# Splitting the first sixteen of 256 indirect embedding loads into two of 64 rows each

## What is computed

```
e = stack([tbl_f[ids[:, f]] for f in range(32)], axis=1)          # 1024 x 32 x 32
x1 = einsum('bpd,pj->bjd', outer(e, e).reshape(b, 32*32, 32), W0)  # 1024 x 128 x 32
x2 = einsum('bpd,pj->bjd', outer(e, x1).reshape(b, 32*128, 32), W1)
z = sum(concatenate([x1, x2], axis=1), axis=-1)                    # 1024 x 256
h = relu(concatenate([z, dense_ctx], axis=1) @ W_top1 + b_top1)
h = relu(h @ W_top2 + b_top2)
y = h @ W_top3
```

## Time and profile before

| what | value |
|---|---|
| time, median of 3 runs | 376.81 us (376.74 to 376.88) |
| the profiled execution: its span, first to last instruction | 597.7 us |
| the profiled execution: a time of its own, beside the span | none is recorded |
| mean granted TensorE clock in it | 0.800 |
| PE, DVE, ACT, POOL busy | 412.6, 203.4, 235.5, 246.5 us |

### The profile page before, as it was taken

The page is one execution under the profiler, slowest core; times in us unless marked ns, Lnnn a source line. Parts: engine busy times, 40 slices in busy tenths (PEclk is TensorE's granted clock), DMA queues, the critical chain, the costliest instruction groups (busy, mean ns, idle before and its releaser), DMA issues.

```text
span 597.7 us, 9512 instructions
## 1 busy us (share of the span) xinstructions
PE 412.6 (69%) x3656; PEld 360.8 (60%) x3656; DVE 203.4 (34%) x834; ACT 235.5 (39%) x774; POOL 246.5 (41%) x262
## 2 busy tenths in 40 slices
PE   5512112874257887877788778687787679999988
PEld 4301001653256776766666667577676668989988
DVE  4200000694723333322333233333332235556510
ACT  3300000662175334522343334433452237676641
POOL 6777772547055444544445554544444440000000
PEclk9755555795589877877787888977787779999999
DMA  8100000000000000000000000000000000000000
GB/s 299 45 14 13 13 13 6 11 3 14 2 10 10 8 10 7 10 8 9 9 9 10 10 10 9 11 8 9 8 10 8 8 10 2 2 2 2 2 2 1
DMA packets 10765, 9.66 MB, mean 16 GB/s; under 512 B 4664, under 2 KB 8896, under 8 KB 10720
## 3 DMA queue, kind: packets, MB, share of 16 engines
q0 software_dynamic: 8192, 4.21, 4.8%
q1 hardware_dynamic: 2528, 4.84, 2.3%
HBM read 9.03 MB, written 0.00 MB: 15 GB/s over the span
## 4 chain that ended last, share of the span: by engine, by line
PE 57%; issue 18%; another core or an unknown queue 11%; DVE 7%; ACT 6%; DMA 1%; SPq 0%; ACTq 0%
PE WA L725 20%; PE QB L697 10%; PE PA L687 8%; PE T L710 4%; DVE RT L421 4%; PE M L738 4%; PE M L757 2%; PE ET L674 2%; ACT eblk L285 2%; ACT TS L285 1%; PE PA L639 1%; PE M L764 1%; PE M L748 1%; ACT RT L285 1%
## 5 line engine op out<-in xcount | busy, mean ns | idle before, releaser
L278 POOL DMA_INDIRECT emb<-in_table,rows x256 | 245.8, 960 | 239.0 <-PE ET L674 165.3
L725 PE MATMUL WA<-TS,RX 128*128 128x128 f32 x896 | 127.0, 301 | 1.0 <-ACT TS L285 1.0
L584 DVE COPY TS<-T 32x64 f32<-32x64 f32 x256 | 55.5, 217 | 200.6 <-PE T L710 184.6
L725 PEld LDWEIGHTS WA<-TS,RX 128*128 128x128 f32 x896 | 119.7, 215 | 6.0 <-issue 6.0
L697 PE MATMUL QB<-eblk,zQ 128*64 128x68 f32 x1024 | 69.1, 243 | 74.3 <-issue 74.0
L697 PEld LDWEIGHTS QB<-eblk,zQ 128*64 128x64 f32 x1024 | 49.9, 146 | 89.8 <-issue 85.8
L552 DVE TENSOR_TENSOR zQ<-ET,eT 128x1024 f32<-128x1024 f32 x32 | 39.2, 1225 | 159.0 <-ACT eT L285 158.9
L687 PE MATMUL PA<-eblk,zP 128*128 128x132 f32 x512 | 80.6, 296 | 5.3 <-issue 3.4
L639 PE MATMUL PA<-sym,TS 128*128 128x272 f32 x64 | 29.4, 552 | 74.5 <-issue 47.3
L687 PEld LDWEIGHTS PA<-eblk,zP 128*128 128x128 f32 x512 | 73.4, 212 | 6.3 <-issue 4.9
L285 ACT ACTIVATE eblk<-ET 32x256 f32<-32x256 f32 x128 | 48.6, 380 | 71.0 <-PE ET L674 66.0
(11 more groups left out here) (87 smaller groups left out, 294.1 us busy)
## 6 DMA issues: line engine op xcount, KB each, us to landing
emb<-in_table,rows POOLq DMA_INDIRECT x256
TS<-in_W SPq DMA_DIRECT2D x8, 256.0 KB, 4.3
wt<-in_W_top SPq DMA_DIRECT2D x2, 512.0 KB
y1w<-in_W_rows SPq DMA_DIRECT2D x1, 448.0 KB
TS<-in_W_rows SPq DMA_DIRECT2D x1, 448.0 KB
sym<-in_W_cols SPq DMA_DIRECT2D x1, 264.0 KB, 2.8
TS<-in_W_cols SPq DMA_DIRECT2D x1, 264.0 KB, 3.1
idc<-in_ids SPq DMA_DIRECT2D x1, 128.0 KB, 2.0
```

The source lines that it names most:

```text
L278: eng.indirect_dma_start(emb[par][:, g, :], None, table, bass.IndirectOffsetOnAxis(rows[:, k, g:g + 1], 0))\
L584: eng.tensor_copy(view(ts[32 * q:32 * q + 32, :, :], P * REST + b0, [[4 * P, 2], [P, 4], [1, 8]]), view(src, q, [[C17, 2], [4, 4], [C33, 8 ...
L725: m = eng.matmul(WA[:, 0:P], C[:, kt, :], TS[k % 2][:, slot_of(kt), :], start=(kt == 0), stop=(kt == KT - 1))
```

## The change

The loads of the first two units (tile 0, units 0 and 1: 16 loads) are each issued as two loads of 64 rows: partitions 0 to 63 with row numbers from `rows`, and partitions 64 to 127 with row numbers from a new tile `upper`. `upper` lies on partitions 0 to 63. It is filled by a third direct load on SyncE's queue, and VectorE adds the table starts to it, behind the making of `rows`. The second load of each pair waits for that sum. Since each load adds 16 to its semaphore, TensorE's waits on these two units count 16 x 8 more.

```
+    HALVED = 2
...
+        upper = sb("upper", [P // 2, HALVED * UG], I32)
...
             eng.dma_start(base[:, :], bases).then_inc(ids_loaded, 16)
+            eng.dma_start(upper[:, :], ids[P // 2:P, 0, 0:HALVED * UG]).then_inc(upper_loaded, 16)
             eng.dma_start(sym[:, :], w0_cols[0]).then_inc(w0_loaded, 16)
...
                     for g in range(UG * unit, UG * unit + UG):
+                        if k == 0 and unit < HALVED:
+                            eng.indirect_dma_start(emb[par][0:P // 2, g, :], None, table,
+                                                   bass.IndirectOffsetOnAxis(rows[0:P // 2, k, g:g + 1], 0))\
+                               .then_inc(gathered[par][unit], 16)
+                            eng.wait_ge(upper_made, 1)
+                            eng.indirect_dma_start(emb[par][P // 2:P, g, :], None, table,
+                                                   bass.IndirectOffsetOnAxis(upper[:, g:g + 1], 0))\
+                               .then_inc(gathered[par][unit], 16)
+                            continue
...
+            eng.wait_ge(upper_loaded, 16)
+            some = view(base[0:P // 2, :], 0, [[0, HALVED * UG]])
+            eng.tensor_tensor(upper[:, :], upper[:, :], some, ALU.add).then_inc(upper_made, 1)
             eng.wait_ge(w0_loaded, 16 * 2)
...
-                eng.wait_ge(gathered[k % 2][unit], 16 * UG * (k // 2 + 1))
+                halves = 16 * UG if k % 2 == 0 and unit < HALVED else 0
+                eng.wait_ge(gathered[k % 2][unit], 16 * UG * (k // 2 + 1) + halves)
```

More of the change, by code:

```diff
@@ L141, in dlrm_cin_tower @@
         ids_loaded = sem("ids_loaded")
+        upper_loaded = sem("upper_loaded")
+        upper_made = sem("upper_made")
         w0_loaded = sem("w0_loaded")
```

## The result

The changed kernel takes 394.73 us (394.59 to 394.94, 4 runs) against 376.85 (376.74 to 377.24, 4 runs): +17.9 us, a ratio of 1.0464 (95% interval 1.0433 to 1.0495). The forecast was 389.0, with a range of 380 to 397.

What follows compares the result with a forecast made beforehand. The prediction took POOL's unbroken row of indirect loads as the bound; 16 more loads add 12.4 us to 376.8, giving 389.2, less some taken up by PE's floor: forecast 389.0, range 380 to 397.

Steps and rivals of the forecast that it cites:

- What bounds the kernel: Whole kernel: POOL's row of indirect loads without a gap sets the end, a floor of 365.0 to 369.9 us.
- unnamed rest of 6.9 to 11.8 us: What the median holds above POOL's floor: time around the span and whatever late signals a timed run has.
- The price of a load of 64 rows: POOL's 16 added loads: bounded by +4.8 and +20.0 us, middle taken, +12.4, a half load about 0.71 + 0.30.
- the likeliest case: Middle cost of a half load on POOL: range 384 to 393 us, chance 0.48.
- a half costs as much as a whole: Rival on POOL's loads: time does not depend on rows, +16.5 to 20 us, 393 to 397, chance 0.20.
- The wait, the direct load, the extra sum: Start of the kernel: wait for `upper` taken as 0, SyncE's load one issue of 0.42 us, VectorE's sum 0.
- What is late next: PE behind units 0 and 1: data 6.2 us later, PE's floor up 10.0, POOL's other 240 loads 12.4 later.
- The two floors: Ends of a run without late signals: 365.0 to 369.9 us by POOL, 363 to 383 by PE.
- Half cost: Rival on POOL's loads: only the idle pieces count, +4.8 us on POOL, 380 to 382, chance 0.16.
- Slack on POOL: Rival: late signals or profiler-made idle pieces leave POOL slack, so the change is hidden, 377 to 380 us, chance 0.12.
- the faster case: Rival on the 23 columns behind unit 0: half loads disturb PE's signals less, at best about 371 us, chance 0.04.

## Why the prediction held, and where its size was off

**What bounds the kernel.** Right, though the profile that I had could not show it directly. The sum was 324.1 for the end of the row, 0 to 4.9 for the landing, 40.9 behind it. The second profile of the same kernel has 332.7 (331.78 + 0.94), 1.4 and 40.9 (375.1 - 334.16). The 8.6 us between 324.1 and 332.7 I had left in an unnamed rest of 6.9 to 11.8 us; they are the loads slowed by VectorE's sums (8.4 us, by the run with the sums replaced). Half of that size stood in a row that I quoted: by the mean of 0.960 the 256 loads take 4.1 us more than by the median of 0.944 that I used. Another 1.8 us lie around the span. The 13 runs beside the second profile have spans of 374.7 to 376.1 us, so they leave no room for late signals such as the first profile had.

**The price of a load of 64 rows.** This is the term that was mis-sized. I had 0.71 + 0.30 and +12.4, the middle between half the cost and the whole; it is 0.903 + 0.30 and +18.6, of which 17.9 show in the time. So the likeliest case was the wrong one, and the rival "a half costs as much as a whole", with 393 to 397 and a chance of 0.20, is what happened. The stated range held the result only because it took in this rival too. By the last sentence of the prediction, which calls it wrong if a half load costs over 0.9 us, it was wrong here. My reading of the packets was right (32 for each load of either size), but I took them for half of POOL's work without a row that says so. The narrow spread of the earlier trace rows, 938 least and 944 median, was the better hint, and I gave it too little weight. The Trainium skill's sentence in DMA: Bandwidth & Descriptors, section Anatomy of one DMA, that many descriptors can be emitted before their cost shows, agrees with the runs: 96 rows more cost 0.077 us of POOL.

**The wait, the direct load, the extra sum.** Taken at 0, and 0 to within about 1 us by the run that keeps them with whole loads. POOL started at 4.00 with the change as without it; PE's first column starts at 7.01 in place of 6.36.

**What is late next.** In the changed kernel PE waits 6.39 us for unit 0's data and 7.42 for unit 1's, and transposes them at 24.45 and 43.81; I had about 25.3 (19.13 and 6.2) and 38.5, with cheaper halves. That the first came out so near is luck: unit 0's last load ends 8.9 us later, not 6.2, but its landing shrank from 4.6 to 1.3 us, and I had left it as it was. The two waits of PE cost nothing of their own: the kernel that splits the last units has neither, and is not faster. That PE's floor would rise somewhat less than POOL's, and not set the end, was right: unit 6's transposes, reached at PE's own pace, come at 100.70 before and 113.92 after the change, 13.2 us later, while POOL's row is 18.1 later.

**The two floors.** I had POOL's 365.0 to 369.9 and PE's 363 to 383 and took POOL's as the bound by judgement. The second profile and the run with 64 loads left out have 375.1 for POOL's and 367.7 for PE's; tile 1 begins at 90.8 in the latter, in the lower part of my 87 to 107. The up to 2 to 3 us that I said PE's floor might take up were not taken up.

**The other rivals.** Half cost falls with the row of half loads. Slack on POOL and the faster case fall with the second profile of before: it has 77.7 us of idle pieces ahead of the loads, waits for no late signal, and yet its own time is that of the other runs.

What stays open is why the first profiled execution of the kernel before took 597.7 us. The same kernel profiled again, and the changed one and its relatives, show nothing of it.

## What to carry to other kernels

Count the indirect loads, not their rows: 32 rows cost 0.87 us of POOL and 128 rows 0.94, with 0.30 ahead of each, so splitting one buys nothing and costs 1.16 us wherever POOL's row is what the last unit waits for. Before a difference is read off a profile, hold its span against the timed median; where they disagree, build the floor of each engine from paces in undisturbed stretches and ask which of them the median can hold. An engine at 67% busy can be the bound while one at 84% waits for it, if the rest of its time are fixed gaps.

## What the runs showed that I had not expected

- One profiled execution can be 222.6 us longer than another of the same kernel (597.7 and 375.1 us of span), while the timed runs of that kernel beside them have medians of 376.81 to 377.42.
- Sums on VectorE with both operands in SBUF stretched indirect loads on POOL from 0.944 us to as much as 2.5, 8.4 us over the kernel. The Trainium skill, SBUF — State Buffer, section Who interferes with whom, tells of a probe in which such sums did not stall DMAs, while copies did, and calls its reason inferred. The loads of this kernel behave otherwise: the run replaced the sums alone, and the slow loads were gone. The same section says that a VectorE instruction with two inputs in SBUF contends with a GpSimd instruction that reads SBUF. The runs agree with that if an indirect load counts as one, since it takes its row numbers from `rows` in SBUF; that this is the reason is not shown.
- PE's wait of 9 to 10 us shortly before the end costs twice: after it the clock stands at the lower level for a while, and the same last stretch takes 43.0 us in place of 41.0 (granted clock 0.50 against 1.00 in its first 4.2 us).
